# Mask slices in the mixture stage, a bias sum on GpSimd, and the decoder stream accumulated in a TensorE bank

## The reference

```
x = x + moe(layernorm(x))                     # layer 1: 8 experts, 2 chosen, GELU
x = x + attention(layernorm(x), ctx)          # layer 2: keys beyond each sequence's length masked
...
# layer 4, a decoder: self attention, cross attention, feed forward; both attentions with a key mask
t = layernorm(t + gelu(t @ fc1_w + fc1_b) @ fc2_w + fc2_b) * ln3_g + ln3_b
x = x + t
# layer 5, ternary: quantise, multiply by weights of -1, 0, 1
x = x + round_clip(layernorm(x) / s) * s @ (tern - 1) + bias
# layer 6: attention with 16 heads of 8; its output bias is l3_bo
x = x + softmax(q k / sqrt(8)) v @ Wo + bo
# layer 7: feed forward with quantised input, weights and hidden values; its output bias is l3_bout
```

## Time and profile before

| | |
|---|---|
| time, median of 3 runs | 1124.57 us (1124.46 to 1126.37) |
| profiled execution, its own time | 1127.0 us |
| its span in the profile | 1125.3 us |
| mean granted clock of TensorE | 0.979 |
| TensorE busy | 994.2 us (88%) |
| VectorE busy | 790.0 us (70%) |
| ScalarE busy | 556.7 us (49%) |
| GpSimd busy | 235.5 us (21%) |

### The profile page before, as it was taken

The page is one execution under the profiler, slowest core; times in us unless marked ns, Lnnn a source line. Parts: engine busy times, 40 slices in busy tenths (PEclk is TensorE's granted clock), DMA queues, the critical chain, the costliest instruction groups (busy, mean ns, idle before and its releaser), DMA issues.

```text
span 1125.3 us, 33301 instructions
## 1 busy us (share of the span) xinstructions
PE 994.2 (88%) x12405; PEld 796.2 (71%) x12405; DVE 790.0 (70%) x1896; ACT 556.7 (49%) x1068; POOL 235.5 (21%) x247
## 2 busy tenths in 40 slices
PE   4778999988999997899989999988999888879887
PEld 4557888866777776788868878766778776556546
DVE  6777767487777776556396677566776668887877
ACT  1543434644655553433456565544656553445533
POOL 4662222122222221422010000000000002235300
PEclk9899999999999998999999999999999999999989
DMA  9300000000000000000000000000000000000001
GB/s 361 148 1 1 0 0 0 1 1 2 1 0 0 0 0 2 1 1 1 1 2 1 0 0 0 1 2 2 0 0 0 1 2 1 1 1 0 1 1 38
DMA packets 5925, 16.21 MB, mean 14 GB/s; under 512 B 729, under 2 KB 4962, under 8 KB 5218
## 3 DMA queue, kind: packets, MB, share of 16 engines
q1 hardware_dynamic: 5858, 15.29, 3.5%
HBM read 14.24 MB, written 1.05 MB: 14 GB/s over the span
## 4 chain that ended last, share of the span: by engine, by line
PE 57%; DVE 15%; issue 13%; DVEq 9%; ACT 3%; POOL 2%; POOLq 0%; ACTq 0%
PE banks L1819 9%; PE banks L1892 5%; PE banks L1864 5%; PE banks L1526 4%; PE banks L973 3%; PE banks L1852 3%; PE banks L1221 3%; PE banks L1569 2%; PE banks L1880 2%; PE banks L1441 2%; PE banks L1643 2%; PE banks L1556 1%; DVE xn L341 1%; PE banks L1609 1%; DVEq L1979 1%
## 5 line engine op out<-in xcount | busy, mean ns | idle before, releaser
L1827 ACT ACTIVATE work<-banks 128x512 f32<-128x512 f32 x128 | 74.9, 600 | 70.6 <-PE banks L1819 70.6
L363 POOL TENSOR_TENSOR rstd<-var,nhalf 128x2 f32<-128x2 f32 x64 | 45.7, 713 | 296.1 <-DVE var L334 288.8
L1422 ACT ACTIVATE work<-work 128x1024 f32<-128x1024 f32 x64 | 67.8, 1060 | 46.6 <-DVEq L1418 29.1
L1819 PE MATMUL banks<-xT_all,weights 128*128 (+1 forms) x384 | 86.2, 380 | 2.3 <-ACT work L1941 1.8
L1975 DVE TENSOR_TENSOR work<-banks,neg_mask 128x512 f32<-128x512 f32 x64 | 40.7, 686 | 63.7 <-PE banks L1852 62.3
L1819 PEld LDWEIGHTS banks<-xT_all,weights 128*128 128x128 f32 x384 | 71.6, 190 | 13.7 <-ACT work L1941 2.6
L1011 ACT ACTIVATE work<-banks,weights 128x256 f32<-128x256 f32 x128 | 53.6, 473 | 54.5 <-PE banks L963 53.7
L1448 ACT ACTIVATE work<-banks 128x512 f32<-128x512 f32 x128 | 68.1, 603 | 11.4 <-PE banks L1441 7.7
L973 PE MATMUL banks<-weights,work 128*128 128x128 f32 x512 | 64.7, 280 | 8.1 <-DVE work L1109 7.6
L973 PEld LDWEIGHTS banks<-weights,work 128*128 128x128 f32 x512 | 62.4, 195 | 12.2 <-ACT work L1011 6.2
L1892 PEld LDWEIGHTS banks<-weights,work 128*128 128x128 f32 x512 | 58.4, 191 | 14.8 <-ACT work L1941 14.8
(11 more groups left out here) (349 smaller groups left out, 2284.6 us busy)
## 6 DMA issues: line engine op xcount, KB each, us to landing
weights<-wpack SPq DMA_DIRECT2D x1, 5381.5 KB, 32.3
weights<-wpack SPq DMA_DIRECT2D x1, 2060.0 KB, 12.9
weights<-wpack SPq DMA_DIRECT2D x1, 2049.0 KB, 17.3
weights<-wpack SPq DMA_DIRECT2D x1, 1160.5 KB, 19.7
x_all<-x_in SPq DMA_DIRECT2D x2, 512.0 KB, 4.8
ctxT_all<-ctxT_in SPq DMA_DIRECT2D x1, 1024.0 KB, 6.1
out<-x_all SPq DMA_DIRECT2D x8, 128.0 KB, 1.8
rows<-rows_in SPq DMA_DIRECT2D x1, 832.0 KB
```

The costliest lines, as they stand in the source:

```text
L1422: act.activation(sm[:, u, :], sm[:, u, :], ACT.Exp, scale=scale).then_inc(h["exp"].sem, 1)
L1819: ins = pe.matmul(bank(ring.bank(f"qk{c}"))[:, j * PT:(j + 1) * PT], wt[:, 2 * (c % 4) + j, :], cols(src, p), start=True, stop=True)
L1827: act.activation(dst.rearrange("p c t -> p (c t)"), bank(ring.bank(f"qk{c}")), ACT.Copy) \
```

## The change

- The two tables are made in eighths of 256 columns. Each pair makes its piece of `neg_len` and of `neg_mask` behind the eviction of `down1`; the last piece of `neg_mask` is made in pair 0, and the last pair signals `converted`.
- In the feed forward, TensorE starts each half of the down product with the identity times the pair of `tok_all`, and accumulates the product on it. VectorE takes statistics and centring from the bank, and no longer adds; it releases the bank (`y_read`) behind the centring.
- The sum of `l3_bo` moves from VectorE to GpSimd, ahead of the second spreading of keys. VectorE waits for it (`bias_summed`) ahead of the first residual of that layer.
- In the first and last steps of the last attention, ScalarE stores both halves of the first turned probabilities ahead of the second exponential.
- At the end, the first part of the last bias stands ahead of the last division, the second ahead of the last residual.

```diff
@@ -1073,7 +1074,7 @@
 
             def vector(v):
 
-                def converts():
+                def casts():
 
                     v.tensor_copy(lensf[:], lens_i)
                     v.tensor_copy(ternw[:], tern_i)
@@ -1081,15 +1082,18 @@
                     v.tensor_scalar(ternw[:], ternw[:], -1.0, None, ALU.add)
                     v.wait_ge(consts_made, 1)
                     v.reduce_sum(headmask8[:], headmask[:].rearrange("p (g j) -> p j g", j=8), AX)
-                    v.tensor_tensor(neg_len[:].rearrange("p (b k) -> p b k", k=S),
-                                    iseq[:, None, :].to_broadcast([P, B, S]),
-                                    lensf[:, :, None].to_broadcast([P, B, S]), ALU.is_ge)
-
-                def masks():
-
-                    v.tensor_scalar(neg_len[:], neg_len[:], -NEG, None, ALU.mult)
-                    v.tensor_scalar(neg_mask[:], mask_u8, -NEG, None, ALU.mult)
-                    v.drain().then_inc(converted, 1)
+
+                def key_masks(p):
+
+                    v.tensor_scalar(cols(neg_mask, p), cols(mask_u8, p), -NEG, None, ALU.mult)
+
+                def masks(p):
+
+                    v.tensor_tensor(cols(neg_len, p).rearrange("p (b k) -> p b k", k=S),
+                                    iseq[:, None, :].to_broadcast([P, 4, S]),
+                                    lensf[:, bass.ds(4 * p, 4)][:, :, None].to_broadcast([P, 4, S]), ALU.is_ge)
+                    v.drain()
+                    v.tensor_scalar(cols(neg_len, p), cols(neg_len, p), -NEG, None, ALU.mult)
 
                 def combine(ring, i, p):
 
@@ -1109,8 +1113,15 @@
                             ins = v.tensor_tensor(prod[:, u, 2 * j:2 * j + 2, :], bk[:, u, :, :],
                                                   comb[:, u, 2 * j:2 * j + 2, None].to_broadcast([P, 2, D]), ALU.mult)
                         ins.then_inc(dve_emptied, 1)
-                        if ring is s.body and isinstance(p, int) and j == 1:
-                            converts()
+                        if j == 1:
+                            if ring is s.body and isinstance(p, int):
+                                casts()
+                                key_masks(PAIRS - 1)
+                            masks(p)
+                            if ring is s.body:
+                                key_masks(p)
+                            if ring is s.last:
+                                v.drain().then_inc(converted, 1)
                     v.drain()
 
                 def step(ring, i, p):
@@ -1122,7 +1133,6 @@
                     combine(ring, i, p)
 
                 combine(s.body, 0, 0)
-                masks()
                 prog[att1][5](v)
                 with v.Fori(1, PAIRS - 1) as p:
                     step(s.body, p, p)
@@ -2108,7 +2118,7 @@
                 pe.wait_ge(*s.emptied(p, "up1"))
                 settle(pe)
                 pe.wait_ge(*y_read.at(p, 1))
-                down_product(pe, w("fc2"), ffn_hT)
+                down_product(pe, w("fc2"), ffn_hT, stream=pair(tok_all, p))
 
             def ternary(p):
                 settle(pe)
@@ -2153,13 +2163,15 @@
                                     start=True, stop=True)
                 ins.then_inc(banks_filled, 1)
 
-        def down_product(pe, weights, hidden, y=None):
+        def down_product(pe, weights, hidden, y=None, stream=None):
             y = ybank if y is None else y
             wv = weights.rearrange("p (c f) -> p c f", f=D)
             for u in range(2):
+                if stream is not None:
+                    pe.matmul(y[:, u, :], ident[:], stream[:, u, :], start=True, stop=False)
                 for c in range(4):
-                    ins = pe.matmul(y[:, u, :], hidden[:, c, u * P:(u + 1) * P], wv[:, c, :], start=(c == 0),
-                                    stop=(c == 3))
+                    ins = pe.matmul(y[:, u, :], hidden[:, c, u * P:(u + 1) * P], wv[:, c, :],
+                                    start=(stream is None and c == 0), stop=(c == 3))
             ins.then_inc(y_filled, 1)
 
         def ffn_scalar_head(act):
@@ -2208,10 +2220,11 @@
             def product_added(p):
 
                 v.wait_ge(y_filled, p + yb(s))
-                v.tensor_tensor(xd, ybank, pair(tok_all, p), ALU.add).then_inc(y_read.sem, 1)
-                v.drain()
-                norm_stats(v, xd, inner)
-                centred_scaled(v, xd, inner, "ln3_g")
+                norm_stats(v, ybank, inner)
+                for u in range(2):
+                    ins = v.scalar_tensor_tensor(xd[:, u, :], ybank[:, u, :], inner[1][:, u, 0:1],
+                                                 rows[:, ROWS.index("ln3_g"), :], ALU.subtract, ALU.mult)
+                ins.then_inc(y_read.sem, 1)
 
             def stream_added(p):
 
@@ -2470,9 +2483,10 @@
                     heads_taken(p - 1)
                 if ring is not s.epi:
                     att3_queries_taken(act, ring, i)
-                store_probs(act, ring, i, 0, halves=(0,))
+                store_probs(act, ring, i, 0, halves=(0,) if ring is s.body else (0, 1))
                 soft_exp(act, p, 1, 8.0 ** -0.5, h3)
-                store_probs(act, ring, i, 0, halves=(1,))
+                if ring is s.body:
+                    store_probs(act, ring, i, 0, halves=(1,))
                 if turn:
                     store_turned(act, g_of(s, p) - 1, p - 2)
                 store_probs(act, ring, i, 1)
@@ -2528,12 +2542,13 @@
                 soft_in(v, ring, i, p, 1, None, h3)
                 if ring is s.epi:
                     values(ring, i, p)
+                if ahead is s.one:
+                    v.wait_ge(bias_summed, 1)
                 end3[0](v, s, p - 1)
                 if ring is not s.epi:
                     values(ring, i, p)
 
             values(s.one, 0, 0)
-            v.tensor_tensor(x_all[:], x_all[:], row("l3_bo", TILES), ALU.add)
             part(s.one, 0, s.body, 0, 1, False)
             with v.Fori(2, PAIRS - 1) as p:
                 part(s.body, p - 2, s.body, p - 1, p, True)
@@ -2544,10 +2559,10 @@
             end3[1](v, s, PAIRS - 2)
             v.drain()
             v.tensor_reduce(amax[:, 5:6], xn[:].rearrange("p u d -> p (u d)"), AX, ALU.max, apply_absolute_value=True)
+            end3[2](v, slice(0, TILES // 2))
             divided(s.epi, 0, "o_last")
-            end3[2](v, slice(0, TILES // 2))
+            end3[2](v, slice(TILES // 2, TILES - 2))
             end3[0](v, s, PAIRS - 1)
-            end3[2](v, slice(TILES // 2, TILES - 2))
             end3[1](v, s, PAIRS - 1)
 
 
@@ -2897,6 +2912,8 @@
                 if s is att3:
                     att3_pool(g, s.one, 0)
                     stage_inputs(g, s, 1)
+                    g.wait_ge(*h3["values"].at(0, 1))
+                    g.tensor_tensor(x_all[:], x_all[:], row("l3_bo", TILES), ALU.add).then_inc(bias_summed, 1)
                     att3_pool(g, s.body, 0)
                     take_root(g, s, 0, 1)
                     stage_inputs(g, s, 2)
```

More of the change, by code:

```diff
@@ L202, in build_program @@
         converted = sem("converted")
+        bias_summed = sem("bias_summed")
         banks_filled = sem("banks_filled")
```

## The result

| | before | after |
|---|---|---|
| median, runs on one chip beside each other | 1124.72 us (1124.46 to 1126.37, 4 runs) | 1111.45 us (1110.1 to 1115.89, 4 runs) |
| ratio | | 0.9882, 95% interval 0.986 to 0.9904 |
| profiled execution: own time, span | 1127.0, 1125.3 us | 1110.67, 1108.6 us |

Sets of the same kernel that were run later beside other kernels had medians of 1112.03, 1110.83 and 1112.3, against 1123.91, 1122.36 and 1124.66 of the kernel before: 11.9, 11.5 and 12.4 less, with ratios of 0.9899, 0.9899 and 0.9888.

The account below looks back on a forecast made before the run. TensorE was read as busiest, with 57% of the chain, but VectorE as carrying most of the changed stretches. 4.0 + 3.3 + 3.2 + 0.6 = 11.1 us off 1124.57 gave 1113.5 us, range 1111.5 to 1117.5 (own range 1111.8 to 1115.2).

Parts of the forecast that it names:

- Masks, 4.0 forecast: First mixture stage: masks made in slices under VectorE's waits, and TensorE keeping its clock in pair 1, save 4.0 us.
- VectorE's 2.4 less: First mixture stage, pair 0: without the two whole multiplications behind the last eviction, VectorE comes 2.4 us sooner.
- The clock's 1.6: Pair 1's third down product: with less idling ahead, TensorE keeps full clock, 1.6 us saved, bounds 0 and 1.6.
- Joined loop, 3.3: Feed forward and ternary loop: TensorE accumulating the decoder stream spares VectorE 0.50 us a pair, 3.3 us; bounds 0.4 and 3.6.
- The rival with TensorE behind: Joined loop: TensorE can't follow, having 0.05 us of margin; 2.9 us less gain, chance 0.17 shared with dearer bank reads.
- Bias sum, 3.2: Opening of the last attention: moving the sum to GpSimd saves 2.3 us of VectorE and 0.9 of TensorE's clock.
- GpSimd's 3.8: Opening of the last attention: the moved bias sum takes GpSimd about 3.8 us, hidden from VectorE.
- Tail, 0.6: End of the kernel: GpSimd's last root runs alone, 0.64 us gained, less up to 0.25 for TensorE's clock; 0.6 taken.
- The clock held in pair 1 and at the turning of the opening: Rival: TensorE's clock stays low in both places, 2.5 us less gain, 1116.0 us; chance 0.20.
- the loop's reads cost nothing: Rival: joined loop's bank reads cost the copy's step; 2.9 us less gain, 1116.4; chance 0.17 shared with TensorE not following.
- the slices were covered: Rival: mixture stage's mask slices lie on the chain in seven pairs, 9.8 us back, 1123.3, no change; chance 0.04.
- nothing left the feed forward loop at the lower clock: Rival: longer accumulation leaves that loop at TensorE's lower clock, five us a pair, 35 in all, slower; chance 0.03.

Follow-up runs that it names:

- b_again: The kernel before, unchanged, run again for a second trace: median 1125.05 us, beside 1123.91 for the kernel before in the same set.
- a_late: The changed kernel with each pair's mask slices behind the eviction of the fourth down product instead of the second: median 1121.98 us.
- a_four: The changed kernel with two more identity products ahead of each down product of the joined loop, output the same: median 1113.82 us.
- a_probs: The changed kernel with the earlier storing of turned probabilities, but VectorE's order of the tail as before: median 1114.42 us.
- a_best: a_probs with both parts of the last output bias between the last division and the residual: median 1112.71 us.
- a_filled2: a_best with eight filler passes instead of four behind the result, and four instead of six ahead of the last feed forward: median 1111.52 us.
- e_bias: The kernel before with only the bias sum moved to GpSimd: median 1120.7 us, ratio 0.9971.
- e_masks: The kernel before with only the masks made in eighths: median 1120.03 us, ratio 0.9962.
- e_ runs: Four kernels, each the kernel before with one part of the change (masks, decoder stream, bias sum, tail): medians 1120.03, 1121.23, 1120.7 and 1123.02 us.
- a_again: The changed kernel, unchanged, run again with a second trace: median 1112.03 us, ratio 0.9899.
- a_notail: The changed kernel with ScalarE's and VectorE's orders of the tail as before: median 1114.93 us.

## Why the prediction came out a little short

**Masks, 4.0 forecast.** The stage is 3.5 to 3.9 shorter in 11 of 13 traces with the edit and 2.2 in the two where pair 0 lost the clock, against 0.1 less to 1.6 more in the five without it. VectorE's 2.4 less came as worked out (the norm of pair 1 is 2.4 sooner). The clock's 1.6 was called an upper bound and isn't one: b_again's stage, 1.3 longer still, lost some 2.9 to it. The slices were costed too dear (0.99, not 1.4), at no consequence. The warning of the Trainium skill (VectorE: DVE Perf Modes, The TRN2 errata) against small tiles is true of the slices' sum; a_late shows what it costs uncovered, and covered it costs next to nothing.

**Joined loop, 3.3.** The loop is 3.2 or 3.3 shorter in all 14 traces with this edit (a_four, with more products in it, aside). Reads from the bank cost no more; the 62 cycles by the same page's table would have made the turn 0.26 us longer, and no row shows them. The rival with TensorE behind did not come, but a_four shows that its margin was real.

**Bias sum, 3.2: a step that failed the other way.** The opening is 3.5 to 3.6 shorter in 11 of the 15 traces with the edit, and 1.9 to 2.0 in the other four, where the clock falls ahead of the turning. VectorE's part was right: the turning starts 12.0 us behind the cut before and 9.85 behind it after, 2.2 against 2.3 forecast. The rest, 1.4, is the clock's, where 0.9 was forecast with 1.3 as the bound. But the prediction gave it to the edit, and it isn't the edit's: three of five traces without the edit have it too. Mean against mean (0.9 shorter without, 3.1 with) the edit is worth 2.2. GpSimd's 3.8 was taken from two instructions of 1024 columns and is 4.53. The Trainium skill (GPSIMD Engine Reference, 3.1 Elementwise — side-by-side cycle accounting) has 4497 ns for just this addition of 2048 columns; the trace agrees, with 4.53 us.

**Tail, 0.6: the step that failed, and the one term that was clearly too small.** The prediction's own path came true: the root at 0.69, and the 0.25 "if TensorE's clock falls sooner" at the turning (0.69 in place of 0.44). The last norm is 0.4 us sooner in the second of the first two traces, and 0.5 on average. What the prediction put at nothing, without a reason, is the six filler passes that the last feed forward waits for: it followed the chain to the last norm and not to the next product. They take 2.84 in place of 4.36 in the first two traces, and 3.2 in place of 4.7 on average. So the tail measured 1.9 between the first two traces, 1.8 by the mean of 8 ends with it against 7 without, and 2.2 and 2.9 by medians within the changed kernel, where 0.6 was forecast.

**The sum.** Taken as differences of means over all the traces, the four terms are 4.2, 3.1, 2.2 and 1.8, together 11.3 (an estimate from the table). The forecast had 4.0, 3.3, 3.2 and 0.6, together 11.1. That these agree is luck: the tail was 1.2 too small and the bias sum 1.0 too large. The four sets say 12.3 by their medians, 1.0 over that estimate, and the first set's 13.3 is 1.0 more again. Both steps are within what medians of a few executions differ by, and no run shows a cause for either. So of the 2.2 us by which the forecast fell short in the first set, the tail's 1.2 is the part with a cause, the bias sum takes 1.0 of it back, and the rest stays open. The lower end of the range lay only 2 us below the forecast. All doubts that were counted pointed to a smaller gain, and the falls of the clock that one execution happened to show were counted as the kernel's own.

**Rivals.** None of them came. The clock held in pair 1 and at the turning of the opening (0.44 in the changed kernel; in a_four, a_probs, a_best and a_filled2 it fell elsewhere in one or both of these stretches, at 1.6 us each), the loop's reads cost nothing, the slices were covered, and nothing left the feed forward loop at the lower clock (1.00 in the window of 943 to 951 us).

## What to carry to other kernels

Where TensorE's clock takes part, follow an edit to the next stretch that TensorE's own products set, past the waits: a fall of the clock in front of fillers can be worth more than it costs, and a gain on VectorE that opens an idle stretch can be lost whole behind it. Before you price anything by the slow places of a trace, take a second trace of the same kernel: they may be that execution's alone, as 4.4 of the 16.7 us between the first two were here. A stream that TensorE can accumulate is a cheap way to take an addition from VectorE, once: of a second pair of such products two thirds came back as time.

## What the runs showed of the hardware

- The length of an idle stretch alone doesn't say whether TensorE's clock falls behind it. It held behind 2.73 and 3.50 us in pair 1 of the mixture stage. Behind the 2.4 us ahead of pair 0 it held in the first trace of before and fell in e_bias, a_four and a_probs. At the opening of the last attention idle stretches of 1.58 and 0.64 us were followed by full clock in the changed kernel (eight passes in 1.06) and by the lower one in a_probs, a_best and a_filled2 (1.71 to 1.92). One fall costs 1.5 to 2.9 us where TensorE's products are waited for, and nothing where VectorE is later anyway (e_masks, opening).
- Where the falls come differs from execution to execution of one kernel. How much of the 8 to 9 us between its fastest and slowest execution that makes isn't shown: of the 35 executions of the kernel before beside the e_ runs, the slowest (1128.32) had a mean granted clock of 0.979 and the fastest (1120.8) one of 0.977.
- Two engines on tensors in memory hold each other up. In a_again the norm of two instructions took 2.28 us beside GpSimd's spreading of the keys, and 0.60 without it (at 996.76). The spreading ended at 981.97, and the norm 0.55 behind it, at 982.52. GpSimd, then VectorE:

```profile
978.20 3.77 POOL L2509 TENSOR_TENSOR work<-work,headmask 128x1024 f32<-128x1024 f32 x2
```

```profile
980.24 2.28 DVE L342 SCALAR_TENSOR_TENSOR xn<-x_all,mv_third,small 128x128 f32<-128x128 f32 x2 [0.21 <-issue]
```

The Trainium skill (SBUF — State Buffer, Who interferes with whom) calls the pair of ports that VectorE and GpSimd share an exclusive lock, and says that a VectorE instruction with two inputs in memory contends with a GpSimd instruction that reads memory. These rows agree. So does the root, a GpSimd instruction: where it started 0.17 us behind the start of a VectorE addition in memory that lasted 0.95 (a_notail), it took 1.33 us and ended 0.55 behind the addition; alone it takes 0.69.
